# Four x1 normalisations from VectorE to GpSimd, outputs one turn later on ScalarE, and a last FFN half in two quarters

## The reference

```python
# x: (16, 2048, 1024); 16 query heads and 2 key/value heads of 64; window of 256
q, k, v = x @ Wq + bq, x @ Wk + bk, x @ Wv + bv
kp, vp = pad(k, 128 rows on both sides), pad(v, 128 rows on both sides)
# row s sees rows s .. s+255 of the padded keys
out = softmax(q . k_win) @ v_win            # no scale
x = layernorm(x + out @ Wo + bo)
W_real, W_imag = unfold(G1_R, G2_R), unfold(G1_I, G2_I)      # 512 x 512 each
real, imag = split(x, 2)
f = concat(real @ W_real.T - imag @ W_imag.T + bias_real,
           real @ W_imag.T + imag @ W_real.T + bias_imag)
x = layernorm(x + f)
```

## Time and profile before

| | |
|---|---|
| median of 3 runs | 491.24 us (491.09 to 491.98) |
| the profiled execution | 491.3 us |
| its span, slowest core (2) | 489.8 us |
| spans of the 8 cores | 484.1 to 489.8 us |
| PE busy in the span | 459.2 us, 94% |
| DVE busy | 390.8 us, 80% |
| ACT busy | 316.8 us, 65% |
| POOL busy | 170.0 us, 35% |
| chain that ended last | PE 82%, DVE 6%, issue 5% |

### The profile page before, as it was taken

How to read it: one execution, slowest core, us unless ns; L and a number is a source line. 1 busy time by engine, 2 the same in 40 slices (tenths; PEclk the granted TensorE clock), 3 DMA queues, 4 the chain that set the end, 5 groups by cost and what they waited for, 6 DMA issues and landing times.

```text
span 489.8 us, 11362 instructions; the slowest of 8 cores (484.1 to 489.8 us)
## 1 busy us (share of the span) xinstructions
PE 459.2 (94%) x3832; PEld 216.9 (44%) x3832; DVE 390.8 (80%) x619; ACT 316.8 (65%) x398; POOL 170.0 (35%) x118
## 2 busy tenths in 40 slices
PE   0698999999999999999999999999999999899994
PEld 0454444444444444444444444444444444344542
DVE  0193678688887988798887988788887888899985
ACT  0136766566776767767676667666766677777653
POOL 8100044343334323443334334432333233333360
PEclk9999999999999999999999999999999999899998
DMA  6999985545664556646664556546642345556333
GB/s 59 160 168 172 217 209 109 108 118 121 150 153 99 140 131 151 144 99 147 151 151 99 134 138 150 136 102 152 151 117 78 111 128 130 153 150 130 87 87 129
DMA packets 82808, 65.15 MB, mean 133 GB/s; under 512 B 67776, under 2 KB 68288, under 8 KB 82752
## 3 DMA queue, kind: packets, MB, share of 16 engines
q1 hardware_dynamic: 75984, 51.17, 40.3%
q0 software_dynamic: 6768, 13.26, 18.4%
HBM read 44.63 MB, written 16.78 MB: 125 GB/s over the span
## 4 chain that ended last, share of the span: by engine, by line
PE 82%; DVE 6%; issue 5%; DMA 3%; ACT 3%; POOL 1%; DVEq 0%; ACTq 0%; POOLq 0%
PE pW L428 22%; PE pW L507 19%; PE pW L493 13%; PE pW L459 9%; PE pS L438 9%; DMA XT<-xt 3%; PE pW L418 3%; PE pW L413 2%; PE pW L476 2%; ACT EX L651 1%; DVE st L805 1%; DVE xb L800 1%; DVE xr L800 1%; PE pS L507 1%; PE pW L402 1%
## 5 line engine op out<-in xcount | busy, mean ns | idle before, releaser
L651 ACT ACTIVATE EX<-pS,shift 128x2048 bf16<-128x2048 f32 x96 | 188.5, 1964 | 58.4 <-PE pS L438 58.4
L376 POOL TENSOR_TENSOR xb<-x,beta_b 128x1024 f32<-128x1024 bf16 x32 | 69.2, 2161 | 159.9 <-DVE x L882 150.9
L428 PE MATMUL pW<-XT,wq_sb 128*128 128x512 bf16 x512 | 120.1, 379 | 0.4 <-DMA XT<-xt 0.2
L507 PE MATMUL pW<-wo_sb,attnT 128*128 128x512 bf16 x496 | 118.2, 384 | 0.0
L384 POOL TENSOR_TENSOR xr<-xr,bo_b 128x1024 f32<-128x1024 f32 x32 | 75.6, 2362 | 121.7 <-DVE EX L777 101.3
L638 ACT ACTIVATE QT<-pW,bq_sb 128x512 bf16<-128x512 f32 x64 | 44.0, 687 | 60.7 <-PE pW L428 59.0
L777 DVE TENSOR_TENSOR EX<-EX,mask_s 128x2048 bf16<-128x2048 bf16 x64 | 80.1, 1252 | 3.3 <-ACT EX L651 3.1
L852 DVE TENSOR_TENSOR xb<-pW,xb 128x1024 f32<-128x1024 f32 x48 | 58.8, 1225 | 17.6 <-PE pW L493 11.2
L507 PEld LDWEIGHTS pW<-wo_sb,attnT 128*128 128x128 bf16 x496 | 45.7, 98 | 60.2 <-issue 14.1
L428 PEld LDWEIGHTS pW<-XT,wq_sb 128*128 128x128 bf16 x512 | 46.0, 98 | 48.4 <-issue 1.8
L459 PEld LDWEIGHTS pW<-VB,EX 128*128 128x128 bf16 x1512 | 50.1, 97 | 27.1 <-issue 26.1
(11 more groups left out here) (77 smaller groups left out, 365.0 us busy)
## 6 DMA issues: line engine op xcount, KB each, us to landing
xr<-x SPq DMA_DIRECT2D x32, 512.0 KB, 3.9
y<-xb SPq DMA_DIRECT2D x31, 512.0 KB, 3.0
XT<-xt POOLq DMA_DIRECT2D x32, 256.0 KB, 5.2
wq_sb<-wq POOLq DMA_DIRECT2D x8, 256.0 KB, 21.8
wo_sb<-wo POOLq DMA_DIRECT2D x4, 512.0 KB, 36.8
bo_b<-bo SPq DMA_DIRECT2D x1, 512.0 KB, 10.5
beta_b<-beta SPq DMA_DIRECT2D x1, 512.0 KB, 5.7
y<-xb SPq DMA_DIRECT2D x2, 256.0 KB, 2.1
```

The source lines that it names most:

```text
L376: gp.tensor_tensor(xb[:, r1 % 4 * D:(r1 % 4 + 1) * D], x1[:, r1 % 2 * D:(r1 % 2 + 1) * D], beta_b, ALU.add).then_inc(gp_b, 1)
L428: i = pe.matmul(p, wq_sb[:, t * 1024 + c * 128:t * 1024 + (c + 1) * 128], rhs_x(g, c), start=c == 0, stop=c == 7)
L507: i = pe.matmul(ps, attnT[:, p % 2 * D + c * 128:p % 2 * D + (c + 1) * 128], wo_sb[:, half * 4096 + c * 512:half * 4096 + (c + 1) * 512], ...
L651: act.activation(EX[:, e0:e0 + 2048], pS, AF.Exp, bias=shift).then_inc(act_e, 1)
```

## The change

The diff, all of it that does something:

- VectorE's turns 28 to 31 lose `x1_norm`. GpSimd does the same tensor_scalar for tiles 25 to 28 (`GP_X1`), behind the wait for `masked(s, 0)` and for ScalarE's `rs1`, and signals with a new semaphore, `gp_x1`, on which its own addition of beta waits, and SyncE's `x1_t` too.
- ScalarE's turns 28 to 31 take `rstd` and `out_norm` of tile `s - 5`, between exponential 1 and exponential 2; tile `s - 4` no longer follows exponential 2. Tile 27 is normalised behind the loop. SyncE stores tile `s - 5` in each of these turns, and 27 behind the loop.
- The last FFN half (half 1 of tile 31) is computed as two quarters of 256 columns, in banks 3 and 0. VectorE takes the statistics of half 0 in two pieces of 256 columns, then residual and statistics of each quarter, into `st3` of 24 columns, and aggregates those.

```diff
@@ wlist: the end
-              (("F", 2 * N2), (1,)), (("F", 2 * N2 + 1), (7,)), (("F", 2 * N1), (2,)), (("F", 2 * N1 + 1), (3,))]
+              (("F", 2 * N2), (1,)), (("F", 2 * N2 + 1), (7,)), (("F", 2 * N1), (2,)), (("E", 0), (3,)), (("E", 1), (0,))]
+    GP_X1 = list(range(Q_END - 3, N4 + 1))
@@ sync
-                if 5 <= s <= Q_END:
+                if s >= 5:
                     store(s - 5)
-                if s >= Q_END:
-                    store(r)
+            store(N4 - 1)
             x1_t(N3)
@@ gpsimd
-                    gp.wait_ge(*x1_done(r1))
                     if i < NT:
                         gp.wait_ge(dve_m, 2 * i + 1)
+                    if r1 in GP_X1:
+                        gp.wait_ge(act_r1, r1 + 1)
+                        gp.wait_ge(d_x1t[r1 % 2], r1 // 2 * 16)
+                        gp.tensor_scalar(x1[:, r1 % 2 * D:(r1 % 2 + 1) * D], xr[:, r1 % 4 * D:(r1 % 4 + 1) * D],
+                                         mv1[:, r1 % 4 * 2:r1 % 4 * 2 + 1], rs1[:, r1 % 4:r1 % 4 + 1],
+                                         ALU.subtract, ALU.mult).then_inc(gp_x1, 1)
+                    gp.wait_ge(*x1_done(r1))
@@ tensor
+            def ffn_quarter(q):
+
+                p = take_w(("E", q))
+                for c in range(8):
+                    w = wit if c < 4 else wrt
+                    i = pe.matmul(p[:, 0:256], x1T[:, N1 % 2 * XW + c * 128:N1 % 2 * XW + (c + 1) * 128],
+                                  w[:, c % 4 * 512 + q * 256:c % 4 * 512 + (q + 1) * 256], start=c == 0, stop=c == 7)
+                i.then_inc(pe_w, 1)
             ffn(N1, 0)
-            ffn(N1, 1)
+            ffn_quarter(0)
+            ffn_quarter(1)
@@ scalar, turns from 28
-                    if s == Q_END:
-                        n_ln += 1
-                        rstd(r - 1, dve_v2, mv2, ln2, rs2, act_r2, n_ln)
-                        out_norm(r - 1)
                     ex(s, 1)
+                    n_ln += 1
+                    rstd(r - 1, dve_v2, mv2, ln2, rs2, act_r2, n_ln)
+                    out_norm(r - 1)
                     ex(s, 2)
-                    n_ln += 1
-                    rstd(r, dve_v2, mv2, ln2, rs2, act_r2, n_ln)
-                    out_norm(r)
-
+
+            rstd(N4 - 1, dve_v2, mv2, ln2, rs2, act_r2, n_ln + 1)
+            out_norm(N4 - 1)
@@ vector, turns from 28
                     masked(s, 0)
-                    x1_norm(r1)
                     f_residual(r, 0)
@@ vector, the end
             f_residual(N1, 0)
-            f_stats(N1, 0)
-            f_residual(N1, 1)
-            f_stats(N1, 1)
+            v.wait_ge(dve_v2, N1)
+            v.wait_ge(*emptied(("F", 2 * N1)))
+            b0 = N1 % 4 * D
+            for q in range(2):
+                v.bn_stats(st3[:, q * 6:(q + 1) * 6], xb[:, b0 + q * 256:b0 + (q + 1) * 256])
+            for q in range(2):
+                u, c0 = ("E", q), b0 + 512 + q * 256
+                v.wait_ge(pe_w, wpos[u] + 1)
+                v.tensor_tensor(xb[:, c0:c0 + 256], bank(u)[:, 0:256], xb[:, c0:c0 + 256], ALU.add).then_inc(dve_w, 1)
+                v.wait_ge(*emptied(u))
+                i = v.bn_stats(st3[:, (2 + q) * 6:(3 + q) * 6], xb[:, c0:c0 + 256])
+            i.then_inc(dve_st, 1)
+            v.wait_ge(dve_st, stat_count(2, N1))
+            v.wait_ge(*out_done(N1 - 4))
+            v.bn_aggr(mv2[:, N1 % 4 * 2:N1 % 4 * 2 + 2], st3).then_inc(dve_v2, 1)
```

More of the change, by code:

```diff
@@ L90, in build_nc @@
     st2 = sb("st2", 12, F32)
+    st3 = sb("st3", 24, F32)
     mv1 = sb("mv1", 8, F32)
@@ L173, in build_nc @@
     gp_b = sem("gp_b")
+    gp_x1 = sem("gp_x1")
     head = [("K", 0), ("V", 0), ("Q", 0), ("Q", 1), ("Q", 2)] + [("G", n) for n in range(4, 8)] + [("Q", n) for n in range(3, 8)]
@@ L209, in build_nc @@
               (("O", 2 * N1 + 1), (4,)), (("F", 2 * N3), (5,)), (("F", 2 * N3 + 1), (0,)), (("T", 1), (6,)),
-              (("F", 2 * N2), (1,)), (("F", 2 * N2 + 1), (7,)), (("F", 2 * N1), (2,)), (("F", 2 * N1 + 1), (3,))]
-    empties = {"G": dve_w, "Q": act_w, "K": act_w, "V": dve_w, "F": dve_w, "O": dve_w, "A": dve_n, "S": act_e, "T": act_w, "H": dve_w}
+              (("F", 2 * N2), (1,)), (("F", 2 * N2 + 1), (7,)), (("F", 2 * N1), (2,)), (("E", 0), (3,)), (("E", 1), (0,))]
+    empties = {"G": dve_w, "Q": act_w, "K": act_w, "V": dve_w, "F": dve_w, "O": dve_w, "A": dve_n, "S": act_e, "T": act_w, "H": dve_w, "E": dve_w}
     wpos, wbank, wempty, wfree = {}, {}, {}, {}
@@ L244, in x1_done @@
             return act_x1, ACT_X1.index(t) + 1
-        return dve_x1, t + 1 - sum(a < t for a in ACT_X1)
+        if t in GP_X1:
+            return gp_x1, GP_X1.index(t) + 1
+        return dve_x1, t + 1 - sum(a < t for a in ACT_X1 + GP_X1)
     def out_done(t):
```

## The result

The changed kernel takes 488.82 us (median of 9 runs, 487.51 to 490.2) against 491.61 us before in the same comparison: ratio 0.9949, 95% interval 0.9929 to 0.9969, so 2.5 us less (1.5 to 3.5), where −5.1 us, 486.1 us, was forecast. Two of the nine executions of the kernel before, 555.92 and 535.96 us, fell into a slower state of the chip and are left out of the ratio. The profiled execution of the changed kernel took 490.2 us.

The account below looks back on a forecast made before the run. VectorE was taken to pace turns 29 to 31 at 11.28 us, TensorE next at 10.30; −5.3 us to the tail and +0.2 for quarters made −5.1, 491.24 to 486.1 us, range 485.4 to 493.3.

Parts of the forecast that it names:

- ScalarE's order: Turn 28: moving tile 23's output behind the second exponential removes TensorE's 1.82 us wait and 1.68 us of slow projection.
- VectorE's turn: Turns 28 to 31: without x1 and the held mask, VectorE's turn falls from 11.28 to 10.19 us.
- The cost of 0.36 by the held mask: VectorE's second mask: waiting for GpSimd's beta addition made it 1.58 us in place of 1.22; this would go.
- The price p of x1 on GpSimd: GpSimd's tensor_scalar for x1: estimated at 1.76 us, between 1.16 from memsets and 2.35 from a two-tensor addition.
- x1 arrives later by p + 0.2 − 0.7: x1 on GpSimd: over 1 us later, but its transposed form is wanted only a turn later.
- room of "over 1 us": Last turn: slack said to be left for the later x1.
- rivals 2 and 3: Second mask waits for x1's end: 488.0 us as forecast's upper end; or then loses port to beta addition: 495.2, chance 0.07.
- Rival 1: Turns 28 to 31: quick x1 lets GpSimd's beta addition shut out the second mask; 492.7 to 494.0 us, chance 0.33.
- The slower side of the forecast: Chance 0.34 that the whole kernel gets slower, from losses at the second mask of turns 28 to 31.
- The slowest core: Tail: −5.3 us on the slow-projection core; others can gain up to 1.7 us less but ended earlier.
- Quarters: Last FFN half: six VectorE operations of 256 columns for three of 512, 0 to +0.4 us, taken as +0.2.
- The clock: Turn 28's output projection: 5.31 us at a lowered clock against 3.63 on core 4, so 1.68 us to win.

Follow-up runs that it names:

- e1: ScalarE's order and the stores alone changed against the kernel before, x1 left on VectorE, last half whole; ratio to before 0.9989.
- e8: e4 with VectorE's first mask of turns 28 to 31 moved behind the first FFN residual and its statistics; ratio to before 0.9906, 486.96 us.
- e10: e3 with GpSimd's x1 over 512 of 1024 columns, so half of x1 is not computed; ratio to before 0.9908.
- e3: The changed kernel with the last FFN half whole again, no quarters; ratio to before 0.9946.
- e9: e3 with one operation in GpSimd's x1, the mean left out; ratio to before 0.9918.
- e2: Only x1 of tiles 25 to 28 moved to GpSimd, against the kernel before; ratio to before 0.9961.
- e5: The kernel before with 15 GpSimd operations on scratch data appended behind its end; only durations read, x1's form 3.78 us.
- e4: e3 with GpSimd starting x1 once ScalarE's rs1 is there and adding beta behind the second mask; ratio to before 0.9931.
- e6: e3 with x1 of tile 25 alone back on VectorE; ratio to before 1.0053.
- e7: The kernel before with only the last FFN half in quarters; ratio to before 1.0029.

## Why the prediction was wrong

The forecast was −5.1 us and the measurement is −2.5. The path was seen rightly, VectorE first and TensorE's 10.3 us a turn behind it; what failed is the price of x1 on GpSimd, and with it the step that let x1T come in time. The 488.8 us lie inside the range of 485.4 to 493.3, but by luck: neither the forecast nor one of the rivals that widened it has the wait that the runs show.

- *ScalarE's order, turn 28.* Right as to the place: the wait of 1.82 us and the slow projection went, the turn is 10.3 us. Right also that this is worth nothing by itself: e1 gives 0.1%.
- *VectorE's turn.* 10.19 us predicted, 10.19 measured in turn 28 of the change, and in e8 and e10, which have no wait in turn 29, in three turns of three. The cost of 0.36 by the held mask went too.
- *The price p of x1 on GpSimd.* This is the step that failed. "From above: the addition of two f32 tensors of the same shape, 2.35 us" was taken as an upper bound because that addition reads more. It is none: the price goes by the operations and not by the inputs, 3.78 us. The estimate of 1.76 was less than half, and p lay outside the whole range I had reasoned about.
- *"x1 arrives later by p + 0.2 − 0.7 ... its transposed form is wanted only a turn later."* This is the second half of the failed step: the lateness was named, but it was set against a room of "over 1 us" for the last turn only and against no number in turn 29. By its own formula it is 3.3 us at p = 3.78, and the wait of 1.5 us says that the room in turn 29 was 1.8. Priced so, it says when TensorE waits: at p over 2.2 us (e3, e9). With 1.76 turn 29 would have none; with 3.78 there are 1.5 us in turn 29, and up to 0.5 more in turn 31. That is the 1.9 us by which A, 48.4, is over 46.5. The wait in turn 31 is not p's alone, for e10 has it at 2.07; the time of the transfer, 3.5 to 5.9 us, was no term of the sum.
- *Rivals 1, 2 and 3* put their loss at the second mask, held by GpSimd. It never was: 1.22 us in all turns. The tensor_scalar had begun 1.6 us or more before it and did not hold it, so the mask that waits for the end of x1 (rivals 2 and 3) does not occur, and where the addition of beta and the mask meet (turn 29 of core 5, and e10) the addition waits. Rival 1 itself asks for p under 1.5 us, which no run has. The slower side of the forecast rested on a place where nothing happened, and the real rival, a late x1T, was not among them.
- *The slowest core.* −5.3 was the price for a core whose projection had been slow. Four of the eight were not slow, and win 4.35 at most (50.85 to 46.5). The ratio of e10, 0.9908 or −4.5 us (−3.7 to −5.3), is the nearest that a run comes to p as predicted; by it the forecast without the quarters, −5.3, would still have been some 0.8 us too deep, or just at the end of the interval.
- *Quarters.* +0.2 predicted, +0.2 up to VectorE's last instruction in both pairs, +0.26 in B between e3 and the change.
- *The clock.* The slow projection of turn 28 was priced, but not that a new wait can bring the same loss back: in the profiled execution, on core 5 the clock fell behind the wait for x1T, and its turn 29 is some 1.6 us longer than with the wait alone. It hit one core of eight, but the slowest core is the metric.

## What to carry to other kernels

A step that moves to another engine has two prices: what it takes there, and when its result is then due. Work out the second as a number (here: x1 must end 3.5 us before TensorE's FFN, so no more than 2.2 us on GpSimd, and the same transfer took up to 5.9 us in other turns), for that number says by itself at which price the gain ends. An upper bound from another kind of instruction is no bound: where no row has the form, measure it or keep the range open. And a wait is not a gain of its own length: the 1.82 us taken away in turn 28 had been the slack of turn 29, and 0.2 us of them were left (e1, and e3 against e2).

## What the runs showed of the hardware

- A GpSimd tensor_scalar of 1024 columns takes 3.78 us with two operations, 2.8 with one, a copy with a cast 1.04, the sum of two tensors 2.34 (e5). That the operation with one input is the dearer one was not foreseen in the prediction.
- Beside a GpSimd tensor_scalar a VectorE mask takes its usual 1.22 us if it starts 1.03 us or more behind it (e4, the change); one that was asked for 0.2 us behind its working start, by estimate, took 2.04 (e5). The tensor_scalar waits for a mask that is already running (4.83 us in e4, 4.81 in e5), and so does an addition (3.23 in the change, 2.54 in e10). A mask that is asked for while an addition of two tensors runs waits nearly for its end (1.58 in the earlier trace rows, 1.53 in e1). The Trainium skill, "SBUF — State Buffer", section "SBUF: two separate sides", says that whichever of the two engines' operations starts first has the shared ports for the whole instruction; that agrees with the additions and the masks, and not with the tensor_scalar.
- From the end of x1 to the first matmul that waits for its transposed form take 3.5 us on most cores, and 4.1 (the change, turn 29), 4.95 (e10, turn 31), 5.07 (e2, turn 30) and 5.9 us (e6, turn 30) on others. What makes the difference was not found.
- Behind one and the same wait TensorE's granted clock fell on some cores and not on others of one execution: behind 1.82 us on 4 of 8 before, 2 of 8 in e7 and 1 of 8 in e2; behind 1.5 to 2.1 us on 1 of 8 in the change (not on the one that waited 2.11) and on none in e3; behind 2.9 to 3.8 us on 6 of 8 in e6. Each time it fell, the turn was some 1.6 to 1.7 us longer than the wait alone made it.
